# A talking-heads attention beside a gate network: logits computed once per head, sent through DRAM and mixed over heads by block-diagonal 64x64-tile products, and the next batch's heads begun in gate layer 2

## The reference, cut to what matters

```python
xn = layernorm(x)
# s: attention with 16 heads of 16 features
q, k, v = split(xn @ Wqkv.T + bqkv)
q, k = rope(q), rope(k)
logits = einsum('bhid,bhjd->bhij', q, k) * SCALE
logits = einsum('bhij,gh->bgij', logits, Wpre)
attn = softmax(logits)
attn = einsum('bhij,gh->bgij', attn, Wpost)
s = (attn @ v) @ Wout.T + bout
# g: two layers; x -> x + local_attention(shift(x)) @ wo, then x -> x + (a * gelu(gate)) @ w2 + b2
g = silu(gate_network(xn))   # 8 heads of 64, windows of 128 tokens, hidden width 682
out = x + s * g
```

## Time and profile before

| | before |
|---|---|
| median of 3 runs | 5094.69 us |
| span of the profiled execution | 5096.0 us |
| TensorE busy | 97% of the span |
| VectorE, ScalarE, GpSimd busy | 67%, 61%, 57% |
| granted TensorE clock | nine tenths or more in all 40 slices |
| moved by DMA | 325.85 MB, mean 64 GB/s |

### The profile page before, as it was taken

How to read it: one execution, slowest core, us unless ns; L and a number is a source line. 1 busy time by engine, 2 the same in 40 slices (tenths; PEclk the granted TensorE clock), 3 DMA queues, 4 the chain that set the end, 5 groups by cost and what they waited for, 6 DMA issues and landing times. The chain is left out here.

```text
span 5096.0 us, 184542 instructions
## 1 busy us (share of the span) xinstructions
PE 4967.6 (97%) x76184; PEld 4084.3 (80%) x76184; DVE 3402.4 (67%) x8316; ACT 3103.6 (61%) x8073; POOL 2880.2 (57%) x2509
## 2 busy tenths in 40 slices
PE   7999999999999999999999999999999999999998
PEld 5887878878888888887887878888888888878886
DVE  7667676666766667666676766767667676676764
ACT  4656665566655666556666556665566665666655
POOL 5546565565655656555565554655546565465654
PEclk9999999999999999999999999999999999999999
DMA  2311112121111211112111211212112112111111
GB/s 86 120 72 66 70 54 75 47 69 64 55 74 46 75 58 55 74 61 68 50 67 62 74 55 53 80 47 74 55 62 70 47 74 78 44 64 70 53 60 30
DMA packets 61263, 325.85 MB, mean 64 GB/s; under 512 B 6416, under 2 KB 23824, under 8 KB 43536
## 3 DMA queue, kind: packets, MB, share of 16 engines
q1 hardware_dynamic: 49632, 297.26, 15.5%
q0 software_dynamic: 10800, 16.78, 1.7%
HBM read 288.33 MB, written 34.08 MB: 63 GB/s over the span
## 5 line engine op out<-in xcount | busy, mean ns | idle before, releaser
L1603 POOL TENSOR_TENSOR q_lo<-q_mix,q_hi 128x512 fp32r<-128x512 f32 x512 | 661.6, 1292 | 886.5 <-ACT q_hi L1059 886.4
L1072 ACT ACTIVATE probs<-bank_S,neg_max 128x512 f32<-128x512 f32 x1024 | 699.3, 684 | 727.7 <-DVE neg_max L1333 630.1
L772 PE MATMUL bank_S<-k_hi,q_lo 128*128 128x512 f32 x2048 | 880.0, 430 | 22.8 <-ACT probs L1072 13.5
L1333 DVE TENSOR_REDUCE neg_max<-bank_S 128x1 f32<-128x512 f32 x1024 | 696.0, 686 | 277.1 <-PE bank_S L774 269.7
L773 PE MATMUL bank_S<-k_lo,q_hi 128*128 128x512 f32 x2048 | 806.7, 394 | 0.5 <-issue 0.5
L774 PE MATMUL bank_S<-k_hi,q_hi 128*128 128x512 f32 x2048 | 806.3, 394 | 0.0
L789 PEld LDWEIGHTS bank_M<-mixer_n,probs 64*64 64x64 f32 x32768 | 534.0, 135 | 151.5 <-issue 132.9
L1598 POOL TENSOR_TENSOR q_mix<-q_rope,w_pre 128x256 f32<-128x256 f32 x1024 | 625.4, 638 | 43.8 <-POOL q_lo L1603 0.4
L789 PE MATMUL bank_M<-mixer_n,probs 64*64 64x64 f32 x32768 | 600.1, 221 | 8.6 <-DVE o_locT_lo L1442 3.4
L1629 POOL TENSOR_TENSOR l_probs<-l_probs,l_inv 128x1024 f32<-128x1024 f32 (+1 forms) x256 | 430.6, 1689 | 265.7 <-DVE l_inv L1436 265.1
L1614 POOL TENSOR_TENSOR inv_norms<-norms_c,minus_half 128x16 f32<-128x16 f32 x128 | 417.1, 3259 | 239.3 <-DVE norms_c L1370 237.5
(11 more groups left out here) (160 smaller groups left out, 11381.3 us busy)
## 6 DMA issues: line engine op xcount, KB each, us to landing
w_qkv_hi<-split_qkv SPq DMA_DIRECT2D x30, 1536.0 KB, 9.7
w_qkv_lo<-split_qkv SPq DMA_DIRECT2D x30, 1536.0 KB, 6.4
w_hi<-split SPq DMA_DIRECT2D x30, 1408.0 KB, 6.2
w_lo<-split SPq DMA_DIRECT2D x30, 1408.0 KB, 6.1
w_hi<-split SPq DMA_DIRECT2D x30, 768.0 KB, 5.1
w_lo<-split SPq DMA_DIRECT2D x30, 768.0 KB, 7.2
w_o_hi<-split_o SPq DMA_DIRECT2D x30, 512.0 KB, 3.7
w_o_lo<-split_o SPq DMA_DIRECT2D x30, 512.0 KB, 4.7
```

Source lines behind the costliest of these rows:

```text
L772: mm(bank[k][:], q_lo[q], k_hi[:, s, :], start=(s == 0), stop=False)
L1072: fn(probs[:, n % PB, :], bank[k][:], ACT.Exp, bias=neg_max[:, n % 2:n % 2 + 1], accum_out=row_sum[:, n % 4:n % 4 + 1]).then_inc(emptied[k ...
L1333: v.tensor_reduce(neg_max[:, n % 2:n % 2 + 1], bank[k][:], AX.X, ALU.max, negate=True)\
L1603: g.tensor_tensor(q_lo[:, c % QB], q_mix[:], q_hi[:, c % QB].bitcast(F32), ALU.subtract)\
```

## The change

**Raw logits per head.** A new step `raw.n.c` (n: one of 4 blocks of 128 queries, c: one of 8 pairs of heads, 32 steps a batch) multiplies q and k of two heads, one in the lower and one in the upper half of the array's rows, each with 48 rows: three stacks of the 16 features that pair high q with high k, low q with high k and high q with low k. Each head's 128x512 logits go to a bank of its own, S0 and S1. ScalarE copies both to `raw_sb` (2 buffers), and SyncE stores these 512 KB to `raw_all` in DRAM. SyncE loads 512 KB for each pair of tiles from there into `raw_mix` (3 buffers, three pairs ahead of their use), now as 8 queries x 16 heads on the partitions.

**Mixing.** `scores.m` stands for a pair of tiles (32 a batch). It is four float32 products in 64x64 tiles of 512 columns with a block-diagonal `w_pre` as the weight; they fill S0 and S1. Maximum and exponential stay per tile. `expand` and `part` are gone, with the multiplication and the splits of q for each pair of tiles.

**q and k.** GpSimd now rotates k too. `split_k` and `split_q` round on ScalarE and subtract on GpSimd; SyncE sends the parts to DRAM (8 transfers) and loads them in the stacked layout: `keys` 6 transfers a batch, `queries` 6 for each block of 128 queries.

**Room.** The head weights, the rope tables and the rotary tables of the gate now lie over other data and are loaded from DRAM again in each batch; the layer 0 `w_qkv_hi` is loaded behind `talk_v`. `v_heads` has 2 buffers, `probs` 4 instead of 3.

**Order.** The steps of the next batch begin in gate layer 2 (step number 1): `talk_k` behind `project.1`, `raw.0.c` around `scores.26` to `scores.29`, `talk_v` just ahead of the `down` steps. The first batch has the same text as the others; in the last one the steps that finish the last batch stand behind everything.

The texts of the order are new as a whole; the diff shows a line of each.

```diff
+STACK = 3 * GD
+HP = 2
+HC8 = GH // HP
+MB = 3
...
-AHEAD = [("norm",), ("scale",), ("x_turn", 0), ("talk_q",), ("talk_k",), ("talk_v",)]
+AHEAD = [("norm",), ("scale",), ("x_turn", 0), ("talk_k",), ("talk_q",), ("split_k",), ("split_q",), ("talk_v",), ("keys",),
+         *(("raw", 0, c) for c in range(HC8))]
 BEHIND = [("bound",), *(("sigmoid", t) for t in range(TW)), ("silu",), ("gated",), ("store",)]
 
 
 def talk_steps():
 
-    steps = [("scores", 0), ("scores", 1)]
+    steps = []
     for m in range(PAIRS):
-        steps += [("scores", n) for n in (2 * m + 2,) if n < TILES] + [("mix", m)]
-        steps += [("scores", n) for n in (2 * m + 3,) if n < TILES]
+        steps += [("scores", m), ("mix", m)]
+    for n in range(1, TW):
+        steps += [("raw", n, c) for c in range(HC8)]
     return steps
 
...
-project.3 hide.1.5 hide.1.4 talk_k talk_q down.1.0 down.1.1 down.1.2 talk_v down.1.3
+scores.0 qkv.0.0 raw.1.0 join.0.0 raw.1.1 mixers.0 bound qkv.0.1 join.0.1 k_turn.0.0 raw.1.2 q_turn.0.0 raw.1.3
...
+        t_k, k_rope = (over(name, shared_at + 4 * j * INNER, [2, N], F32) for name, j in (("t_k", 2), ("k_rope", 4)))
+        k_hi, k_lo = (over(name, shared_at + 4 * j * INNER, [2, N]) for name, j in (("k_hi", 2), ("k_lo", 4)))
...
+        raw_all = nc.dram_tensor("raw_all", (TW, P, GH, N), F32, kind="Internal").ap()
...
+            def talk_v(step):
+                for kind in ("talk_k", "talk_q", "talk_v"):
+                    sp.wait_ge(filled["S1"], now.fill((kind,), "S1"))
...
+                else:
+                    sp.wait_ge(qkv_spilled, 32 * LAYERS)
+                    sp.dma_start(w_qkv_hi[:].bitcast(F32), split_qkv[0, 0]).then_inc(qkv_loaded, 16)
...
+            def keys_in(step):
+                sp.wait_ge(k_spilled, now.at(k_spilled, 64))
+                if not now.first:
+                    sp.wait_ge(filled["S1"], now.fill(("raw", TW - 1, HC8 - 1), "S1", ago=1))
+                for hp in range(HP):
+                    for i, part in enumerate((0, 0, 1)):
+                        at = hp * SEEN + i * GD
+                        sp.dma_start(keys[at:at + GD].bitcast(F32), spilled_k[part, hp].rearrange("s d c j -> (s d) c j"))\
+                            .then_inc(keys_loaded, 16)
+
...
+                sp.wait_ge(q_spilled, now.at(q_spilled, 64))
+                if not now.first:
+                    sp.wait_ge(filled["S1"], now.fill(("raw", TW - 1, HC8 - 1), "S1", ago=1))
+                queries_in(0)
+
+            def raw_mix_in(b, m):
+                slot, count = raw_slot(b, m)
+                n, at = m // (PAIRS // TW), m % (PAIRS // TW) * 2 * RI
+                for i in range(SB):
+                    sp.wait_ge(raw_stored[i], per[id(raw_stored[i])] * b + 16 * HC8 // SB * (n + 1))
+                sp.dma_start(raw_mix[:, slot], raw_all[n, at:at + 2 * RI].rearrange("(t i) h j -> (i h) t j", t=2))\
+                    .then_inc(raw_loaded[slot], 16)
+
+            def raw(step, n, c):
+                if not c and not now.first:
+                    for m in range((n + 1) * PAIRS // TW - MB, (n + 1) * PAIRS // TW):
+                        slot, count = raw_slot(now.b - 1, m)
+                        sp.wait_ge(raw_loaded[slot], count)
+                for k in ("S0", "S1"):
+                    sp.wait_ge(emptied[k], now.fill(step, k))
+                sp.dma_start(raw_all[n, :, HP * c:HP * (c + 1), :], raw_sb[:, c % SB]).then_inc(raw_stored[c % SB], 16)
+                if c == HC8 - 1:
+                    if n < TW - 1:
+                        queries_in(n + 1)
+                    if n == 0 and now.first:
+                        for m in range(MB):
+                            raw_mix_in(0, m)
...
+            def scores(step, m):
+                sp.wait_ge(filled["S1"], now.fill(step, "S1"))
+                if m + MB < PAIRS:
+                    raw_mix_in(now.b, m + MB)
+                elif now.b < B - 1:
+                    raw_mix_in(now.b + 1, m + MB - PAIRS)
...
+            def raw(step, n, c):
+                if not c:
+                    pe.wait_ge(queries_loaded, now.at(queries_loaded, 96 * (n + 1)))
+                    pe.wait_ge(keys_loaded, now.at(keys_loaded, 96))
+                for k in ("S0", "S1"):
+                    if now.was_filled(step, k):
+                        pe.wait_ge(emptied[k], now.fill(step, k) - 1)
+                for hp in range(HP):
+                    rows = slice(hp * SEEN, hp * SEEN + STACK)
+                    mm(bank[f"S{hp}"][:], queries[rows, c, :], keys[rows, c, :], start=True, stop=True)\
+                        .then_inc(filled[f"S{hp}"], 1)
+
+            def scores(step, m):
+                slot, count = raw_slot(now.b, m)
+                pe.wait_ge(raw_loaded[slot], count)
+                if now.first and not m:
+                    pe.wait_ge(tables, 1)
+                for k in ("S0", "S1"):
+                    if now.was_filled(step, k):
+                        pe.wait_ge(emptied[k], now.fill(step, k) - 1)
+                for half in range(2):
+                    for r in range(RH):
+                        rows = slice(r * (P // RH), (r + 1) * (P // RH))
+                        last = mm(bank[f"S{r}"][half * (P // 2):(half + 1) * (P // 2), :], w_pre[rows, :],
+                                  raw_mix[rows, slot, half, :], start=True, stop=True)
+                        if half:
+                            last.then_inc(filled[f"S{r}"], 1)
...
-                if c >= QB:
-                    act.wait_ge(filled["S1"], now.fill(("scores", (c - QB + 1) * ET - 1), "S1"))
...
+            def raw(step, n, c):
+                at = HC8 // SB * n + c // SB
+                if c >= SB or n or not now.first:
+                    act.wait_ge(raw_stored[c % SB], now.at(raw_stored[c % SB], 16 * at))
+                for hp in range(HP):
+                    act.wait_ge(filled[f"S{hp}"], now.fill(step, f"S{hp}"))
+                    fn(raw_sb[:, c % SB, hp, :], bank[f"S{hp}"][:], ACT.Copy).then_inc(emptied[f"S{hp}"], 1)
...
-            def expand(step, c):
...
-                for s in range(2):
-                    q = q_rope[:, s, c * ET * RI:(c + 1) * ET * RI]
-                    g.tensor_tensor(q_mix[:, s].rearrange("p m (i g) -> p (m i) g", g=GH), q[:, :, None].to_broadcast(shape),
-                                    w_pre[:, None, :].to_broadcast(shape), ALU.mult).then_inc(q_mixed, 1)
...
-    o["w_pre"] = np.repeat(i["L0_attn_Wpre"].T, RI, axis=0)
+    pre = np.zeros((RH, HI, GH, HI, GH), i["L0_attn_Wpre"].dtype)
+    for q in range(HI):
+        pre[:, q, :, q, :] = i["L0_attn_Wpre"].T
+    o["w_pre"] = pre.reshape(P, HI * GH)
```

More of the change, by code:

```diff
@@ L30 @@
 PAIRS = TILES // 2
-PB = 3
+PB = 4
 GR = 4
@@ L268, in banks_of @@
     kind = step[0]
-    if kind == "scores":
-        return [f"S{step[1] % 2}"]
+    if kind in ("raw", "scores"):
+        return ["S0", "S1"]
     if kind == "mix":
@@ L1013, in split_qkv_hi @@
                 act.wait_ge(raw_qkv_loaded, 16 * (l + 1))
+                if not l:
+                    act.wait_ge(heads_spilled, 64)
+                    for kind in ("talk_k", "talk_q", "talk_v"):
+                        act.wait_ge(filled["S1"], now.fill((kind,), "S1"))
                 if l:
```

561 lines of the change are left out of this document (320 added, 241 removed).

## The result

The changed kernel takes 5321.23 us (median of 4 runs, 5313.31 to 5326.68), the kernel before 5095.0 us beside it. The ratio is 1.044, with a 95% interval of 1.0425 to 1.0455: 4.4% slower, where 6.9% faster was forecast, and outside the range of 4550 to 5040 us. The profiled execution of the changed kernel has a span of 5315.1 us.

A forecast was written before the change was run, and what follows sets the result against it. TensorE was taken as the bound: 266 us of work plus 13 and 10 us of S-bank waits gave a 289 us period; 96 + 22 + 3 + 16 x 289 = 4745 us, 6.9% faster, range 4550 to 5040.

The forecast's parts named there:

- TensorE's sum, 266 us: TensorE's work a batch: 309 us, less 88 for old logits, plus 29 mixing, 7 per-head logits, 6 and 3 tile-form changes.
- Rival D: The matmul tiles do not run together on TensorE: period 362 us, total 5900 us; chance 0.02.
- Banks and queues, 23 us a batch: TensorE waits for banks S0 and S1: 13 us from too-short intervals, 10 us from busy engines and strict queues.
- the hold of a mixing step: Each mixing step keeps S0 and S1 for 3.4 us, from its matmuls through maximum and exponentials until TensorE starts again.
- Rival B: S banks and strict queues take it all: at 0.7 us more wait a step, period 324, total 5305 us; chance 0.10.
- short intervals: Of 67 intervals between S-bank steps, 23 hold less TensorE work than the banks' hold, costing 13 us a batch together.
- Transfers, "I cost them at nothing in the steady state": DMA traffic of 62.4 MB a batch, engines some 57% busy, adds 0 us to the steady period.
- the cover of the mix loads: Loads of raw_mix run three pairs ahead, about 27 us, against 3.7 us for a 512 KB load.
- rival C: The round trip through DRAM is the bound: at a sustained 190 GB/s, period 328, total 5370 us; chance 0.04.
- Start and end, 96 + 22 + 3: First qkv matmul at 96 us, first batch 22 us above steady, last batch -13 and +16 us.

The follow-up runs named there:

- both traffics cut: Changed kernel with raw stores, raw_mix loads, q and k spills, keys and queries moving one partition from batch 2 on: 5055 us.
- added traffic: Kernel before the change plus 64 DRAM-to-DRAM transfers of 512 KB a batch in the first 15 batches: 5174.17 us, ratio 1.0161.

## Why the prediction was wrong

*TensorE's sum, 266 us: right.* The work at full clock is 265.8. Two steps in the timeline (start us, us, engine, line) show its new terms:

```profile
888.04 0.50 PE L906 MATMUL bank_S<-keys,queries 48*128 48x512 f32 x2
888.47 1.16 PE L937 MATMUL bank_M<-mixer_n,probs 64*64 64x64 f32 x64
889.86 1.09 PE L920 MATMUL bank_S<-raw_mix,w_pre 64*64 64x512 f32 x8 [0.22 <-ACT raw_sb L1222]
890.87 0.48 PE L964 MATMUL bank_M<-w_out,oT 128*128 128x256 f32 x1
```

A raw step takes 0.43 us with its change of form: of the 512 pairs, 510 start less than 20 ns apart, so the row halves run together, as the Trainium skill ("TensorE: Matmul & The Clock Gate", Part 3: Packing small matmuls) has it; the trace agrees, for this number format too. The mixing takes 1.01 us (0.9 and 0.09 forecast). Rival D is out.

*Banks and queues, 23 us a batch: right, a little low.* 13.8 at the S banks and 13.0 elsewhere. One sum was off: the terms for the hold of a mixing step give 3.5 us, not 3.4. Rival B gave 5305 us, near the time, but for a cause that did not act: on top of the 13 us of short intervals it needed 0.5 to 0.7 us for each of 64 steps, 32 to 45 us a batch, and all waits ahead of S steps together are 13.8.

*Transfers, "I cost them at nothing in the steady state": the step that failed.* The amount was right (997.59/16 = 62.3 MB a batch, 62.4 forecast), so was the busy share of the engines (57% in the steady part), and so was the cover of the mix loads, which TensorE awaits once, 10.4 us in the first batch; rival C is out. But the step asked only who waits for the data. The same engines carry TensorE's instructions, 604 packets for 150,320 matmuls and weight loads, and pauses for late packets cost 17.6 us a batch (1.8 before the change, 5.5 with both traffics cut). The traces of cut and of added traffic show it.

*Clock: a term put at nothing, without a reason.* The forecast let TensorE idle for some 23 us a batch and kept the clock of a kernel that idles for 5. The loss is 12.5 us; even with both traffics cut it is 6.8.

The sum is then 266 + 27 + 18 + 12 = 323 us.

*Groups of the page* that bear on the banks (xcount | busy, mean ns | idle before; issues: KB each, us to landing):

```profile
L920 PE MATMUL bank_S<-raw_mix,w_pre 64*64 64x512 f32 x4096 | 598.5, 643 | 92.2 <-ACT probs L1236 45.0
L1222 ACT ACTIVATE raw_sb<-bank_S 128x512 f32<-128x512 f32 x1024 | 555.7, 598 | 149.9 <-PE bank_S L906 145.7
...
L906 PE MATMUL bank_S<-keys,queries 48*128 48x512 f32 x1024 | 261.9, 501 | 217.8 <-ACT probs L1236 85.4
...
raw_all<-raw_sb SPq DMA_DIRECT2D x512, 512.0 KB, 3.3
raw_mix<-raw_all SPq DMA_DIRECT2D x512, 512.0 KB, 4.4
...
w_qkv_hi<-split_qkv SPq DMA_DIRECT2D x30, 1536.0 KB, 9.4
...
keys<-spilled_k SPq DMA_DIRECT2D x96, 256.0 KB, 10.5
```

A copy of a raw bank takes 0.598 us, as the row used for it had (0.59). The mix loads land in 4.4 us, the `w_qkv` load in 9.4, keys in 10.5.

*Start and end, 96 + 22 + 3: low.* The first qkv matmul is at 106.9 us, the first batch costs 38 above steady and the last 10: 155 in place of 121. The first raw step waits until 79 us for the keys.
